# Attention with 16 heads: the order of an iteration redone on all engines, and the products with values in two groups of eight heads

## The reference

```python
x = x + tanh(g_xattn[0]) * L0_xattn(layernorm(x), ctx, ctx, wq, wk, wv, wo)   # 16 heads of 16, softmax
x = x + tanh(g_ffn[0])   * L0_ffn(layernorm(x), ...)                          # ternary weights, relu squared
x = x + tanh(g_xattn[1]) * L1_xattn(ctx, layernorm(x))                        # dynamic time warping
x = x + tanh(g_ffn[1])   * L1_ffn(layernorm(x), w1, b1, w2, b2)

# inside L0_xattn, per head h of 16 (dk_h = dv_h = 16)
scores = einsum('bhqd,bhkd->bhqk', q, k) / sqrt(256)
attn = softmax(scores, axis=-1)
out = einsum('bhqk,bhkd->bhqd', attn, v)
```

## Time and profile before

| | |
|---|---|
| median of three runs | 1793.09 us |
| the profiled execution | 1793.27 us, span 1791.5 us |
| PE busy | 1369.3 us, 76% |
| DVE busy | 1488.4 us, 83% |
| ACT busy | 1145.1 us, 64% |
| POOL busy | 644.3 us, 36% |
| attention phase | to about 1060 us of the span |

### The profile page before, as it was taken

One profiled execution on the slowest core, in us unless ns is written; L12 is line 12 of the kernel. 1 busy time (PEld: TensorE's weight loads), 2 busy tenths in 40 slices (PEclk: granted clock), 3 DMA queues, 4 the chain that ended last, 5 costly groups with the idle time before them and its releaser, 6 DMA issues. The chain is left out here.

```text
span 1791.5 us, 37525 instructions
## 1 busy us (share of the span) xinstructions
PE 1369.3 (76%) x11461; PEld 1064.1 (59%) x11461; DVE 1488.4 (83%) x4194; ACT 1145.1 (64%) x2463; POOL 644.3 (36%) x1094
## 2 busy tenths in 40 slices
PE   4799999999999999999999984233232005898996
PEld 3588888888888888888888764000000003566664
DVE  7678888888888887888878753999998998999995
ACT  4477777777777777777777752243334003999997
POOL 3233343433434334343343323100000003777785
PEclk8899999999999999999999996555555556999999
DMA  6444544445444454444444312222220003223221
GB/s 175 116 139 128 152 127 131 130 125 149 127 133 131 124 147 127 133 134 124 143 127 139 82 42 57 71 60 61 57 41 6 0 0 93 67 95 101 89 78 48
DMA packets 322942, 179.56 MB, mean 100 GB/s; under 512 B 93793, under 2 KB 318193, under 8 KB 322802
## 3 DMA queue, kind: packets, MB, share of 16 engines
q1 hardware_dynamic: 322802, 178.07, 35.6%
HBM read 122.91 MB, written 50.33 MB: 97 GB/s over the span
## 5 line engine op out<-in xcount | busy, mean ns | idle before, releaser
L741 ACT ACTIVATE pts<-s 128x512 f32<-128x512 f32 x512 | 281.7, 613 | 85.9 <-PE s L484 85.9
L1035 DVE TENSOR_REDUCE nmax<-s 128x2 f32<-128x512 f32 x512 | 327.3, 681 | 7.7 <-PE s L467 6.5
L1148 POOL TENSOR_TENSOR r<-rl 128x512 f32<-128x512 f32 x128 | 133.1, 1040 | 224.6 <-ACT rl L771 181.7
L467 PE MATMUL s<-kst,qst 96*128 96x256 bf16 x1024 | 164.2, 276 | 22.4 <-DMA qst<-q_parts_dram 9.7
L484 PE MATMUL s<-qst,kst 128*128 128x256 bf16 x1024 | 158.0, 276 | 1.4 <-ACT pts L741 0.8
L1426 PE MATMUL gate<-diag,one 128*128 128x512 f16 x35 | 21.2, 607 | 172.0 <-DVE left L1517 172.0
L771 ACT ACTIVATE rl<-wb,fscl 128x256 f32<-128x256 f32 x256 | 108.0, 477 | 64.7 <-PE wb L570 64.7
L566 PE MATMUL wb<-x2l,wfcT 128*128 128x256 f32 x512 | 143.4, 302 | 0.7 <-ACT dd L793 0.7
L498 PE MATMUL oacc<-pts,vw 128*32 128x256 f32 x2048 | 137.9, 387 | 1.3 <-ACT pts L741 1.2
L567 PE MATMUL wb<-x2h,wfcT 128*128 128x256 f32 x512 | 132.6, 281 | 0.0
L433 PE MATMUL wb<-wprT,r2l 128*128 128x256 f32 x512 | 129.3, 292 | 2.8 <-DVE r2l L1004 2.8
(11 more groups left out here) (304 smaller groups left out, 4629.8 us busy)
## 6 DMA issues: line engine op xcount, KB each, us to landing
kst<-k_parts_dram SPq DMA_DIRECT2D x384, 64.0 KB, 2.6
qst<-q_parts_dram SPq DMA_DIRECT2D x384, 64.0 KB, 2.4
k_parts_dram<-kp SPq DMA_DIRECT2D x32, 384.0 KB, 5.2
q_parts_dram<-qp SPq DMA_DIRECT2D x32, 384.0 KB, 3.1
xin<-in_x_dram SPq DMA_DIRECT2D x32, 256.0 KB, 3.1
cT_raw<-in_ctx_T_dram SPq DMA_DIRECT2D x32, 256.0 KB, 5.4
xres<-in_x_dram SPq DMA_DIRECT2D x32, 256.0 KB, 4.6
cin<-in_ctx_dram SPq DMA_DIRECT2D x32, 256.0 KB, 4.7
```

The source lines that it names most:

```text
L467: last = pe.matmul(s1[h % 2][:, t, :], qst[b.p][0:MAXROW, h, t * P:t * P + P], kst[b.p][0:MAXROW, h, :], start=True, stop=True)
L741: act.activation(pt[h % (2 * HPG)], s2[h % 2][:], ACT.Exp).then_inc(e["expd"], 1)
L1035: v.tensor_reduce(nmax[:, T * h:T * h + T], s1[h % 2][:], AX.X, ALU.max, negate=True)\
L1148: pool.tensor_tensor(r2[:], rl[:, k % 2], rl[:, k % 2], ALU.mult)\
```

## The change

The 16 heads of values are now done as two halves of eight heads (two of the old groups back to back); `values(b, half)` waits once, for eight exponentials and an empty bank, and signals once. `copy_group(b, half)` empties the whole bank in one copy of 512 columns. Where ACT and turn_o waited for groups they wait for halves, so `exps` of heads 8 to 15 wait for all of the first half. The call lists of TensorE, ACT, DVE and POOL are reordered:

```diff
-            def values(b, g):
+            def values(b, half):
 
-                w("expd", NH * b.n + HPG * (g + 1), NH * NB)
+                w("expd", NH * b.n + NH // 2 * (half + 1), NH * NB)
...
-                w("o_cp", NG * b.n + g, NG * NB)
-                for t in range(T):
-                    for j in range(HPG):
-                        last = pe.matmul(oacc[HW * j:HW * j + HW, g % 2, :], vw[b.p][:, t, HPG * g + j, :],
-                                         pt[(HPG * g + j) % (2 * HPG)][:, t, :],
-                                         start=(t == 0), stop=(t == T - 1))
+                w("o_cp", 2 * b.n + half, 2 * NB)
+                for g in range(2 * half, 2 * half + 2):
+                    for t in range(T):
+                        for j in range(HPG):
+                            last = pe.matmul(oacc[HW * j:HW * j + HW, g % 2, :], vw[b.p][:, t, HPG * g + j, :],
+                                             pt[(HPG * g + j) % (2 * HPG)][:, t, :],
+                                             start=(t == 0), stop=(t == T - 1))
                 last.then_inc(e["av_mm"], 1)
 # TensorE's list, from out_proj on
+                if there(i):
+                    scores2(i, 4, 6)
                 if there(a):
                     queries(a)
                 if there(i):
-                    values(i, 0)
-                    scores2(i, 4, 6)
+                    scores2(i, 6, 8)
                 if there(s):
                     values_proj(s)
-                if there(i):
-                    scores2(i, 6, 8)
+                if there(y):
+                    turn_y(y)
                 if there(s):
                     scores1(s, 6, 8)
...
-                if there(y):
-                    turn_y(y)
+                if there(i):
+                    values(i, 0)
+                    scores2(i, 8, 10)
                 if there(z):
                     turn_xh2(z)
-                if there(i):
-                    values(i, 1)
...
                 if there(i):
-                    scores2(i, 8, 10)
+                    scores2(i, 10, 12)
...
-                if there(i):
-                    values(i, 2)
-                    scores2(i, 14, 16)
+                if there(z):
+                    fc(z, 2)
                 if there(s):
                     scores1(s, 14, 16)
-                if there(z):
-                    fc(z, 2)
-                if there(i):
-                    values(i, 3)
+                if there(i):
+                    values(i, 1)
                 if there(s):
                     max_transpose(s)
 # ACT
                 for h in range(lo, hi):
                     w("s2_mm", NH * b.n + h + 1, NH * NB)
-                    w("av_mm", NG * b.n + h // HPG - 1, NG * NB)
+                    w("av_mm", 2 * b.n + h // (NH // 2), 2 * NB)
...
-            def copy_group(b, g):
-                w("av_mm", NG * b.n + g + 1, NG * NB)
-                w("o_t", 2 * (b.n - 1) + g // 2 + 1, 2 * NB)
-                act.activation(osb[:, g, :], oacc[:, g % 2, :], ACT.Copy).then_inc(e["o_cp"], 1)
+            def copy_group(b, half):
+                w("av_mm", 2 * b.n + half + 1, 2 * NB)
+                w("o_t", 2 * (b.n - 1) + half + 1, 2 * NB)
+                act.activation(osb[:, 2 * half:2 * half + 2, :], oacc[:], ACT.Copy).then_inc(e["o_cp"], 1)
 # DVE's list
+                if there(s):
+                    maxima(s, 0, 2)
                 if there(a):
                     k_remainder(a)
-                if there(s):
-                    maxima(s, 0, 2)
...
+                if slots:
+                    w("ln_rstd", norms(i, 1), 2 * NB + 5)
+                if there(y):
+                    ln3(y)
                 if there(z):
                     residual1(z)
...
                 if there(a):
                     q_remainder(a)
+                if there(y):
+                    y_low(y)
                 if there(z):
                     w("ln_rstd", norms(i, 2), 2 * NB + 5)
                     ln2(z)
+                if there(s):
+                    maxima(s, 6, 8)
+                if there(z):
+                    low_half(z)
                 if there(nx):
                     ln1(nx)
 # POOL's list
                 rstd(i)
-                if there(z):
-                    x1_rstd(i, z)
                 if there(y):
                     halves(y)
+                if there(z):
+                    x1_rstd(i, z)
```

More of the change, by code:

```diff
@@ L486, in scores2 @@
                     last.then_inc(e["s2_mm"], 1)
-            def values(b, g):
-                w("expd", NH * b.n + HPG * (g + 1), NH * NB)
-                if g == 0:
+            def values(b, half):
+                w("expd", NH * b.n + NH // 2 * (half + 1), NH * NB)
+                if half == 0:
                     if at(b, 0):
@@ L494, in values @@
                     w("vw_cp", b.n + 1)
-                w("o_cp", NG * b.n + g, NG * NB)
-                for t in range(T):
-                    for j in range(HPG):
-                        last = pe.matmul(oacc[HW * j:HW * j + HW, g % 2, :], vw[b.p][:, t, HPG * g + j, :],
-                                         pt[(HPG * g + j) % (2 * HPG)][:, t, :],
-                                         start=(t == 0), stop=(t == T - 1))
+                w("o_cp", 2 * b.n + half, 2 * NB)
[5 more added lines that the diff above has]
+                                             start=(t == 0), stop=(t == T - 1))
                 last.then_inc(e["av_mm"], 1)
             def turn_o(b, half):
-                w("o_cp", NG * b.n + 2 * half + 2, NG * NB)
+                w("o_cp", 2 * b.n + half + 1, 2 * NB)
                 if half == 0:
@@ L638, in iteration @@
                 if there(i):
-                    scores2(i, 10, 12)
+                    scores2(i, 12, 14)
                 if there(s):
@@ L646, in iteration @@
                 if there(i):
-                    scores2(i, 12, 14)
+                    scores2(i, 14, 16)
                 if there(s):
                     scores1(s, 12, 14)
-                if there(i):
-                    values(i, 2)
-                    scores2(i, 14, 16)
+                if there(z):
+                    fc(z, 2)
                 if there(s):
                     scores1(s, 14, 16)
-                if there(z):
-                    fc(z, 2)
                 if there(i):
-                    values(i, 3)
+                    values(i, 1)
                 if there(s):
@@ L730, in values_copy @@
                     act.wait_ge(e["pool_set"], VALUES_SET)
-                w("v_mm", b.n + 1), w("av_mm", NG * (b.n - 1), NG * NB)
+                w("v_mm", b.n + 1), w("av_mm", 2 * (b.n - 1), 2 * NB)
                 for t in range(T):
@@ L816, in iteration @@
                     put_proj(0), put_proj(1), put_proj(2), put_proj(3)
+                if there(i):
+                    exps(i, 4, 6)
                 if there(a):
@@ L819, in iteration @@
                 if there(i):
-                    copy_group(i, 0)
-                    exps(i, 4, 8)
+                    exps(i, 6, 8)
+                if there(s):
+                    values_copy(s)
                 if there(y):
                     yT_copy(y)
-                if there(s):
-                    values_copy(s)
+                if there(a):
+                    middle_part(a, "q_rem", qr, qp, "q_parts_mid")
+                if there(i):
+                    copy_group(i, 0)
                 if there(z):
@@ L829, in iteration @@
                     half_copy(y)
-                if there(a):
-                    middle_part(a, "q_rem", qr, qp, "q_parts_mid")
-                if there(i):
[L833 to L837, removed]
-                if there(z):
-                    low_copy(z)
                 if there(i):
@@ L842, in iteration @@
                 if there(z):
+                    low_copy(z)
+                if there(y):
+                    distance(y)
+                if there(i):
+                    exps(i, 10, 12)
+                if there(ct):
+                    ctx_high(ct)
+                if there(z):
                     relu(z, 0)
                 if there(i):
-                    exps(i, 10, 12)
+                    exps(i, 12, 14)
                 if there(z):
@@ L849, in iteration @@
                 if there(i):
-                    exps(i, 12, 14)
+                    exps(i, 14, 16)
                 if there(z):
                     square(z, 1)
[L853 to L856, removed]
                     relu(z, 2)
@@ L859, in iteration @@
                 if there(i):
-                    copy_group(i, 3)
+                    copy_group(i, 1)
                 if there(z):
@@ L1181, in iteration @@
                 rstd(i)
+                if there(y):
+                    halves(y)
                 if there(z):
                     x1_rstd(i, z)
-                if there(y):
-                    halves(y)
                 if there(a):
```

## The result

The changed kernel takes 1801.23 us in the median of six runs (1799.09 to 1802.41), the kernel before 1793.85 beside it (1792.79 to 1795.07): a ratio of 1.0040, 95% interval 1.0027 to 1.0053. It is slower, where 1768 was forecast, and outside the range.

The account below looks back on a forecast made before the run. TensorE bounds the attention phase. Walking its new order, 1.54 us gone less 0.69 of new waits is 0.85 a period (31.85 to 31.00): -23.0 over 27 periods, -2.2 in five other iterations, -25.2, giving 1768 us, range 1761 to 1775.

Parts of the forecast that it names:

- Two groups for four: Values on TensorE: two seams of 0.22 us between groups go, -0.44 us a period.
- rival 2: The seam between values groups saves nothing: -0.41 us a period, 11 us, 1782; chance 0.12.
- Gap (a): TensorE's wait at scores1(2,4) for DVE's second maximum goes with maxima(0,2) moved ahead: -0.30 us a period.
- gap (c): TensorE's wait at L570 in fc(0) for DVE's lowt goes with low_copy before distance: -0.42 us a period.
- The wait at the ones matmul: New TensorE wait in products for half_copy, which ACT does after xh2_copy: +0.36 us a period.
- The one at scores1(14,16): New TensorE wait at scores1 of head 15 for DVE's maxima: +0.16 us a period.
- Gap (b): TensorE's wait at the xh transposes for DVE's xh goes: -0.38 us a period, with 0.3 us to spare.
- Before fc(0): New TensorE wait until ACT's distance has read the bank that fc(0) overwrites: +0.11 us a period.
- before max_transpose: New TensorE wait at max_transpose, for the end of DVE's last maxima: +0.06 us a period.
- The other five iterations: Iterations where the pipeline fills and empties gain the two seams alone: -2.2 us in all.
- Rival 3: On POOL x1_rstd comes late behind halves, so turn_xh2 waits 1.41 us: +0.56 a period, 1806; chance 0.12 with anything like it.
- Rival 1: Fewer new waits: only that at the ones matmul remains, 1759 us, or none at all, 1749; chance 0.18.

Follow-up runs that it names:

- e4: The kernel before with one move on DVE, maxima(0,2) ahead of k_remainder; 1781.75 us, ratio 0.9943 to the kernel before.
- e1: The changed kernel with one wait added: POOL starts the q part only when DVE has finished xh; 1786.82 us, ratio 0.9974 to the kernel before.
- e7: The kernel before with DVE's ln1 (xhat) moved behind maxima(6,8), where POOL does the q part; 1814.99 us, ratio 1.0116 to the kernel before.
- e11: e10 with load_ctx_products first in SP's list; 1754.74 us, ratio 0.9783 to the kernel before.
- e10: e9 with DVE's two low_squares put behind maxima(12,14) and maxima(14,16); 1758.50 us, ratio 0.9809 to the kernel before.
- e9: e1 with turn_half ahead of turn_xh2, half_copy ahead of xh2_copy and distance ahead of low_copy; 1770.46 us, ratio 0.9872 to the kernel before.
- e3: The changed kernel with x1_rstd ahead of halves again on POOL, as before the change; 1784.73 us, ratio 0.9957 to the kernel before.
- e8: The changed kernel with POOL's q part as two instructions of 256 columns instead of one of 512; 1788.40 us, ratio 0.9968 to the kernel before.
- e5: e1 with turn_half ahead of turn_xh2 on TensorE and half_copy ahead of xh2_copy on ACT; 1778.85 us, ratio 0.9922 to the kernel before.

## Why the prediction was wrong

**What was right.** TensorE set the time. *Two groups for four*: two blocks of 1.93 save the 0.44 to a few hundredths, and rival 2 is out. The Trainium skill's rule that a change of tiling mode drains TensorE and a change of tiles does not (TensorEngine Tiling (Array Packing), "Key Properties") agrees with 1.93. *Gap (a)* and *gap (c)* are gone as worked out, (a) shown alone by e4. The wait at the ones matmul came as walked: 1.77 from the first xh transpose to L543, forecast 1.76. The one at scores1(14,16) was 0.21 for 0.16.

**The step that failed** is *Gap (b)*, "-0.38, with 0.3 us to spare". Its chain was right to the start of ln2. The error is the length of the next row: xh was taken at the 0.73 of the earlier trace rows, a length it has only when no large POOL instruction is under way at its start. The change moves ACT's middle part and with it POOL's q part 3.4 us earlier, and the walk has no line on that; of the k part, which moves too, it says that no gap waits for it, "nothing". That asks who waits for the moved work and not what the moved work runs beside. The gap did not go: TensorE waits 0.46 for xh, where it waited 0.30 before and was to wait 0. The term is thus not -0.38 but a small loss. e1 undoes it alone and gives 0.47 a period; e7 makes the same overlap alone and loses. (By its own rows the gap was worth 0.36, 0.30 and 0.66 for 0.60, and not 0.38; that changes nothing.)

**Two terms were too small.** Before fc(0) 0.32 instead of 0.11, before max_transpose 0.23 instead of 0.06. In both the operand was there on time, and TensorE took longer to start. Distance ended at 519.64 and L567 started at 519.89 (ACT):

```profile
518.80 0.84 ACT L791 ACTIVATE dd<-wb,aa 128x256 f32<-128x256 f32 x2
```

and DVE's last maxima ended at 527.88, L474 started at 528.12:

```profile
526.60 1.28 DVE L1032 TENSOR_REDUCE nmax<-s 128x2 f32<-128x512 f32 x2
```

That is 0.25 and 0.24, where the walk had 0.05, the handover of hrows to L543. Why stays open. At these two places the code has further waits, long met, behind the one that releases, and at L543 it has none; but the transposes of xh have two such waits as well and started 0.06 behind the end of xh (515.07, 515.13), so their number doesn't explain it.

**The sum, again.** 31.00, and 0.54 at xh (0.08 of it drift before that point), 0.21 at fc(0), 0.17 at max_transpose, 0.03 else: 31.95, as measured. Against 27 x 0.85 forecast that is the whole of the steady part. The other five iterations were to give 2.2 and cost 6.2. At the tail the load took most of it, as e11 shows (3.8 us, measured on e10). At the head the trace has low_rank waiting 1.53 us for ACT's x2h where it waited 0.82. No run took the head apart; with the two copies moved in e9 that stretch is as short as before (third transposes of `on` at 146.08; 146.30 before, 148.57 in the changed kernel, 147.79 in e1). So the step that failed is the largest single term and not all of the miss of 33 us: 14 at xh, 10 at the two small terms, 8 at head and tail. e1, without the wait for xh, still takes 1786.8, over the range.

**The rivals.** Rival 3 had the right place and sign, a loss before xh on POOL's account, and the wrong mechanism: x1_rstd was 0.35 early. Rival 1 failed by the same row as the forecast.

## What to carry to other kernels

Before moving an instruction of POOL, look at what DVE runs in its new place, not only at who waits for its result: one DVE row an iteration in SBUF that fell under a 1.2 us POOL instruction cost 12 us here, half of what the change was to bring, and one semaphore wait mended it. A row's length holds for the neighbours that it had; when the neighbours change, bound it by the rows of the same form that ran beside such work. Take waits off together that stand one behind the other, since each alone is largely replaced by the next.

## What the runs showed of the hardware

- A DVE tensor_scalar of 128x256 floats in SBUF takes 405 ns. Started under a POOL instruction of 128x512 or 128x256 in SBUF (the q part, cDl, cTl) it ended 0.15 us after that instruction's end, wherever at least 0.3 us of it was left: 28 xh rows of the changed kernel had on average 1.10 us of the q part left and took 1.25, three had 1.20 of cDl left and took 1.35; in e3, 27 xhat rows had 0.85 left and took 1.00. With about 0.1 us left (24 xhat rows of e1 under cDl) a row took 0.41, as when free.
- Other DVE rows weren't lengthened: in the changed kernel 204 maxima from PSUM that started under a long row of POOL took 673 to 692 ns, free ones 675 to 693; in the kernel before, 60 statistics rows of 128x256 in SBUF that started under the k part took 412 on average, two free ones 414; one yTl each of e1 and e8 that started under cDl took 692 and 691, free ones 692.
- POOL's power of 128x2 didn't hold a DVE row up (31 yn rows of 408 ns with 0.64 us of it left), but grew itself beside it, from 0.71 to 0.80. For the steps of halves only the second can be read: they had 0.15 us or less left when xh started, too little for a hold to show.
- TensorE started 0.05 to 0.06 us after the end of what it waited for at L543 and at xh, 0.10 at low_rank in e5, 0.24 and 0.25 at max_transpose and fc(0).
